# Decoder on one core: the row maxima of the heads of 8 taken off inside the score product

## The reference

```
scores = q @ k.T * scale            # 512 queries x 512 or 77 keys
p      = softmax(scores, axis=-1)   # exp(scores - max) / sum
out    = p @ v
```

## Time and profile before

| | us |
|---|---|
| median of 3 runs | 2002.5 |
| lowest and highest | 2000.7, 2007.37 |
| the profiled execution | 1997.6 |
| its span, first to last instruction | 1995.8 |

### The profile page before, as it was taken

The page is one execution under the profiler, slowest core; times in us unless marked ns, Lnnn a source line. Parts: engine busy times, 40 slices in busy tenths (PEclk is TensorE's granted clock), DMA queues, the critical chain, the costliest instruction groups (busy, mean ns, idle before and its releaser), DMA issues. The chain is left out here.

```text
span 1995.8 us, 23570 instructions
## 1 busy us (share of the span) xinstructions
PE 1566.4 (78%) x8740; PEld 718.1 (36%) x8740; DVE 1134.8 (57%) x2827; ACT 610.3 (31%) x839; POOL 131.8 (7%) x156
## 2 busy tenths in 40 slices
PE   1798659994666888885978997985988479994984
PEld 0332334441233433444433323352436223343342
DVE  5685544446966666644455854545454556744445
ACT  1265332223314023321432651411221124541331
POOL 1000000001000500000000000000000103321000
PEclk9799769996978999996997997886986778997687
DMA  4000000003000000000010000000010000000000
GB/s 187 0 2 1 1 1 0 0 0 124 0 1 1 21 22 2 1 1 1 0 75 18 1 1 0 1 1 1 0 63 0 1 0 1 1 1 1 1 1 11
DMA packets 4081, 27.37 MB, mean 14 GB/s; under 512 B 384, under 2 KB 2432, under 8 KB 2944
## 3 DMA queue, kind: packets, MB, share of 16 engines
q1 hardware_dynamic: 2912, 25.35, 3.2%
q10 hardware_dynamic: 1056, 0.52, 0.1%
HBM read 25.34 MB, written 0.52 MB: 13 GB/s over the span
## 5 line engine op out<-in xcount | busy, mean ns | idle before, releaser
L704 ACT ACTIVATE big<-banks 128x1024 f32<-128x1024 f32 (+2 forms) x320 | 294.2, 958 | 427.8 <-PE banks L507 260.2
L602 DVE TENSOR_REDUCE maxima<-banks 128x1 f32<-128x512 f32 (+4 forms) x640 | 362.5, 603 | 100.9 <-PE banks L476 94.2
L503 PE MATMUL banks<-big 32*128 32x512 f32 (+6 forms) x1280 | 259.5, 656 | 16.8 <-DVE negmaxT L615 16.4
L476 PE MATMUL banks<-big 32*128 32x77 bf16 (+6 forms) x1024 | 161.2, 306 | 30.3 <-DVE maxima L602 18.3
L537 PE MATMUL banks<-big,v_heads 128*9 128x512 f32 (+7 forms) x1024 | 164.3, 585 | 5.8 <-ACT heads_out L657 2.9
L342 POOL TENSOR_TENSOR rstd<-mean_var,minus_half 128x4 f32<-128x4 f32 x46 | 46.9, 1020 | 1645.8 <-DVE mean_var L317 1645.8
L1110 DVE TENSOR_TENSOR big<-big,banks 128x512 f32<-128x512 f32 (+1 forms) x88 | 60.5, 687 | 130.5 <-PE banks L1058 125.2
L1085 ACT ACTIVATE big<-banks 128x512 f32<-128x512 f32 (+1 forms) x120 | 71.7, 597 | 200.6 <-PE banks L1055 200.6
L1068 PE MATMUL banks<-big,moe_weights 128*128 128x512 f32 (+1 forms) x240 | 123.0, 593 | 2.8 <-DVE big L1107 1.5
L476 PEld LDWEIGHTS banks<-big 32*128 32x128 bf16 (+1 forms) x1024 | 58.0, 100 | 166.3 <-DVE maxima L602 102.9
L503 PEld LDWEIGHTS banks<-big 32*128 32x128 f32 (+3 forms) x1280 | 77.9, 187 | 79.6 <-ACT big L704 36.2
(11 more groups left out here) (368 smaller groups left out, 2246.1 us busy)
## 6 DMA issues: line engine op xcount, KB each, us to landing
moe_weights<-in_moe SPq DMA_DIRECT2D x1, 4896.0 KB, 22.1
moe_weights<-in_moe SPq DMA_DIRECT2D x1, 4864.0 KB, 15.0
moe_weights<-in_moe SPq DMA_DIRECT2D x1, 3264.0 KB, 10.6
moe_weights<-in_l3x SPq DMA_DIRECT2D x1, 3072.0 KB, 10.2
late_weights<-in_l2x SPq DMA_DIRECT2D x1, 2048.0 KB, 8.1
moe_weights<-in_l SPq DMA_DIRECT2D x1, 1234.0 KB, 13.2
rows<-in_rows SPq DMA_DIRECT2D x1, 1152.0 KB, 8.1
late_weights<-in_turned SPq DMA_DIRECT2D x1, 1152.0 KB, 17.3
```

Of the source, the lines that this page charges most:

```text
L476: last = nc.tensor.matmul(RING[n % NR][:, x * klen:x * klen + last_key(t)], q[rows, t * P:(t + 1) * P], ks[rows, 0:last_key(t)], start=Tru ...
L503: nc.tensor.matmul(SC[pair % 2][0:size, j % 2, n0:S], ks[rows, i * P:i * P + size], q[rows, n0:S], start=True, stop=False)
L602: nc.vector.tensor_reduce(dst, src, AX_X, ALU.max).then_inc(ring_free.up(), 1)
L704: nc.scalar.activation(E[pair % NEP][0:size, :, n0:S], SC[pair % 2][0:size, :, n0:S], ACT.Exp, scale=scale).then_inc(exp_ready.up(), 1)
```

## The change

Each place of 32 rows gets a ninth row: row 8 of the keys holds ones, row 8 of the queries gets the negative maximum in float32, so the score product itself takes the maximum off. The four `pick` products of each round are gone for heads of 8 (320 products in 80 rounds), and `score_ready` is raised by the second score product of each pair. `negmax` is one DVE instruction that writes float32 into every 32nd column of `c.RW`; the four turned tiles are float32; `move_negmax` adds the whole turned bank to the queries' tile in place instead of copying bfloat16. POOL clears `c.RW` at the start of each such attention, and the first `negmax` of a stage waits for that. The ones come from a biased copy (`ninth`), from padded bias vectors, or, in layer 0's attention, from three strided clears at the start. The other head sizes keep their way.

```diff
@@ row_attention @@
+    room_cleared is a further counter
@@ turn_negmax @@
-        to = RING[n % NR][:, 0:S // 2].bitcast(BF16)
+        to = RING[n % NR] if turned else RING[n % NR][:, 0:S // 2].bitcast(BF16)
         for t in range(ST):
-            last = nc.tensor.transpose(to[:, t * P:(t + 1) * P], c.NM[:, g % 2, t, :], c.ident_bf[:])
+            negmax_tile, unit = (c.RW[:, g % 2, t, :], c.ident) if turned else (c.NM[:, g % 2, t, :], c.ident_bf)
+            last = nc.tensor.transpose(to[:, t * P:(t + 1) * P], negmax_tile, unit[:])
@@ scores @@
-            nc.tensor.matmul(SC[pair % 2][0:size, j % 2, n0:S], ks[rows, i * P:i * P + size], q[rows, n0:S], start=True, stop=False)
-        for j in range(HB):
+            last = nc.tensor.matmul(SC[pair % 2][0:size, j % 2, n0:S], ks[rows, i * P:i * P + size], q[rows, n0:S], start=True, stop=turned)
+            if turned and j % 2:
+                last.then_inc(score_ready.up(), 1)
+        for j in range(0 if turned else HB):
@@ negmax @@
+        if turned:
+            row = c.RW[:, g % 2].rearrange("p t (j w) -> p t j w", j=HB)[:, :, :, 8]
+            if g == 0:
+                dve.wait_ge(room_cleared.sem, room_cleared.at(1))
+            nc.vector.tensor_scalar(row, m, -1.0, None, ALU.mult).then_inc(negmax_ready.up(), 1)
+            return
@@ move_negmax @@
+        if turned:
+            q = queries(*groups[g])
+            nc.vector.tensor_tensor(q, q, RING[n % NR][:, :], ALU.add).then_inc(ring_free.up(), 1)
+            return
@@ POOL's program of row_attention @@
+            if turned:
+                nc.gpsimd.memset(c.RW, 0.0).then_inc(room_cleared.up(), 1)
@@ cross_kv @@
-        bias = None if bk is None else bk[:, k:k + 1]
+        bias = c.ninth[:] if bk is None else bk[:, k:k + 1]
@@ the first block @@
+                nc.vector.tensor_copy(c.ninth[:], c.m("ninth"))
...
-                nc.gpsimd.memset(c.big3(4 * TOK, 4 * TOK), 0.0)
+                key_places = c.big3(4 * TOK, 4 * TOK).rearrange("p (n d) -> p n d", d=32)
+                nc.gpsimd.memset(key_places[:, :, 0:8], 0.0)
+                nc.gpsimd.memset(key_places[:, :, 8], 1.0)
+                nc.gpsimd.memset(key_places[:, :, 9:32], 0.0)
```

More of the change, by code:

```diff
@@ L159 @@
     "moe0": [("w1T", P, L0E * L0HID), ("w3T", P, L0E * L0HID), ("w2T", P, L0E * 3 * P)],
-    "const": [("ident", P, P), ("later", P, P), ("later_t", P, P), ("half_later", P, 2 * P), ("half_ident", P, P // 2), ("pick_id", 96, 32), ("pick", P, 4 * P)],
+    "const": [("ident", P, P), ("later", P, P), ("later_t", P, P), ("half_later", P, 2 * P), ("half_ident", P, P // 2), ("pick_id", 96, 32), ("pick", P, 4 * P), ("ninth", P, 1)],
     "mid": [("iota", P, 32), ("same_head", P, P), ("ctxT", CTX, B * SK), ("L1_WdtT", P, P), ("L1_WBT", P, 16), ("L1_WCT", P, 16), ("L1_A_log", P, 16),
@@ L428, in row_attention @@
     NM = c.NM.rearrange("p z t (j r) -> p z t j r", j=HB)
-    (ring_ready, ring_free, negmax_ready, score_ready, exp_ready, value_ready, out_moved, inverse_ready, masked_ready, cleared,
+    (ring_ready, ring_free, negmax_ready, score_ready, exp_ready, value_ready, out_moved, inverse_ready, masked_ready, cleared, room_cleared,
      dve_step) = (counter(c, n) for n in (
          "ring_ready", "ring_free", "negmax_ready", "score_ready", "exp_ready", "value_ready", "out_moved", "inverse_ready",
-         "masked_ready", "cleared", "dve_step"))
+         "masked_ready", "cleared", "room_cleared", "dve_step"))
     filled, emptied = itertools.count(), itertools.count()
@@ L1924, in decoder @@
         c.pick_id = c.sb("pick_id", [96, 32], BF16)
+        c.ninth = c.sb("ninth", [P, 1])
         c.minus_half = c.sb("minus_half", [P, 8])
@@ L2056, in constants @@
         "half_later": np.concatenate([f > 64 * z + p % 64 for z in range(2)], axis=1),
+        "ninth": p % 32 == 8,
         "half_ident": p % 64 == np.arange(64)[None, :],
@@ L2070, in by_rows, with apart @@
     return w.reshape(k, P, -1).transpose(1, 0, 2).reshape(P, -1)
-def apart(w):
+def apart(w, ninth=0.0):
     out = np.zeros((w.shape[0], HEADS, 32), np.float32)
+    out[:, :, 8] = ninth
     out[:, :, 0:8] = w.reshape(w.shape[0], HEADS, 8)
@@ L2142, in lay_out @@
     for name, n in col_names():
-        v = a[name] if n == 1 or a[name].size > P else apart(a[name][None, :])[0]
+        v = a[name] if n == 1 or a[name].size > P else apart(a[name][None, :], 1.0 if name in ("L1_xattn_bk", "L2_attn_bK") else 0.0)[0]
         if v.shape[0] < P:
```

## The result

The changed kernel took 1984.8 us (median of 4 runs, 1982.7 to 1985.1) and the kernel before 2002.6 in the same comparison (4 runs, 2000.7 to 2007.4): a ratio of 0.9905, 95% interval 0.9887 to 0.9924. Faster, by 17.8 us; the forecast was 1988.7 with a range of 1979 to 2000. The profiled execution took 1985.1, with a span of 1983.3 for 1995.8 and a mean granted clock of 0.862, as before. The two spans differ by 12.5 only, because the profiled execution of the kernel before was 5 us faster than its median and that of the changed kernel was not.

What follows compares the result with a forecast made beforehand. With 512 keys DVE was taken to bound group boundaries and the ACT-PE loop plain rounds; 77-key rounds were nearly gapless on PE. Terms -17.0 (512 keys) and +3.2 (77 keys) gave -13.8, so 1988.7 us, range 1979 to 2000.

Steps and rivals of the forecast that it cites:

- The loop through ACT and PE: Plain 512-key rounds: exponentials need only their own pair, so the loop falls from 3.19 to 2.22 us, under DVE's 2.58.
- A sign that I had named: 512-key rounds: ACT's idle before the exponentials would fall under 0.5 us, from 1.24.
- The group of 512 keys: Four 512-key rounds, score start to next group's score start: 12.34 us for 13.33, a gain of 0.99.
- The first passage: First group-to-group step of a 512-key stage, partly at the low clock: taken to gain 1.0 us.
- Five passages: The steady group-to-group steps of a 512-key stage: taken to gain 5.0 us together.
- the seventh passage: Last group-to-group step of a 512-key stage, a bare chain of maxima, float32 tiles and add: taken to gain 1.05 us.
- rival B, the ring: 512 keys: the three-bank ring makes PE wait for DVE, halving the gain to 0.5 per group; about 1996.7 us, chance 0.15.
- The turned maxima in float32: Four float32 tiles add 0.26 to 0.36 us of PE time per group, covered at 512 keys with 0.05 to spare.
- 77 keys: Short stages: a longer chain to the scores costs 0.21 or 0.32 us a round, 1.6 per stage, +3.2 for two.
- rival C: PE's clock falls within the stages, about 1.9 us more per low round; 15 such rounds give about 2017 us; chance 0.08.
- the argument against it: Claim that the clock would hold because the changed loop leaves PE with smaller gaps, not larger.
- Set-up and POOL: Strided clears at the start and POOL's 0.9 us clear in each stage: hidden or nearly so, taken as 0.

Runs made afterwards that it cites:

- e10: The kernel before plus extra, unused score products ahead of the first turned maxima in all four 77-key attentions, nothing else changed: 1976.5 us, ratio 0.987.
- e9: The changed kernel plus extra, unused score products ahead of the first turned maxima in all four 77-key attentions: 1963.7 us, ratio 0.9838.
- e4: The kernel before, all `pick` products kept, but each pair's put right behind its own score products (heads of 8 only): 1989.8 us, ratio 0.9926.
- e1: The changed kernel with the change kept only in the two 512-key attentions, the 77-key ones in their old way: 1984.1 us, ratio 0.9901.
- e7: The changed kernel with the negative maxima as two bfloat16 rows instead of one float32 row, the add kept: 1993.7 us, ratio 0.9962.
- e6: The changed kernel plus the first group's four score products issued twice more at the start of the two short 77-key stages: 1985.4 us, ratio 0.9911.

## Why the prediction was right, point by point

**The loop through ACT and PE.** Right. The exponentials need only their own pair (at 103.19 they start, while the second pair's products end at 104.01), they follow 1.18 after a round's scores (104.93 to 106.11, forecast 1.1), and with the late signal the loop returns. A sign that I had named failed: ACT's idle time doesn't fall under 0.5 but stays at 0.95 in that round, for DVE and PE now set the pace and ACT has time. One more row of the kernel before bears on the reason that was given, beside the earlier trace rows:

```profile
106.50 0.38 PE L507 MATMUL banks<-negmaxT,pick 32*128 32x512 bf16 x2
```

These are the first pair's `pick` products, and yet the exponential that they signal starts at 107.64, after the second pair's scores (106.98 and 0.59). The Trainium skill ("TensorE: Matmul & The Clock Gate", Part 3) says that matmuls start and end in program order. The wait agrees in respect of the ends; the starts in the records don't (106.50 stands before 106.98, the other way round in the program).

**The group of 512 keys.** Right to 0.02 in the group worked through. Here the whole of layer 0's attention by the starts of the turned maxima; first the kernel before:

```profile
82.79 0.59 PE L488 MATMUL banks<-ident_bf,negmax 128*128 128x128 bf16 x4
...
98.97 0.40 PE L488 MATMUL banks<-ident_bf,negmax 128*128 128x128 bf16 x4
...
165.25 0.40 PE L488 MATMUL banks<-ident_bf,negmax 128*128 128x128 bf16 x4
...
178.53 0.40 PE L488 MATMUL banks<-ident_bf,negmax 128*128 128x128 bf16 x4
```

and the changed one:

```profile
82.56 1.09 PE L492 MATMUL banks<-ident,inverses 128*128 128x128 f32 x4
98.29 0.66 PE L492 MATMUL banks<-ident,inverses 128*128 128x128 f32 x4
...
160.05 0.66 PE L492 MATMUL banks<-ident,inverses 128*128 128x128 f32 x4
171.92 0.66 PE L492 MATMUL banks<-ident,inverses 128*128 128x128 f32 x4
```

The first passage gave 0.45 (16.18 to 15.73) where I took 1.0: at the low clock, which lasts to about 94, the passage was mis-sized. Five passages gave 4.5 (66.28 to 61.76) for 5.0; the seventh passage 1.4 (13.28 to 11.87) for 1.05; what follows, to ACT's last copy, 1.1 for 1.5; the start 0.2. Together 7.7 for 8.5. The order of causes that was named (DVE bounds a group, ACT and PE alternate beneath it) holds; rival B, the ring, doesn't appear.

**The turned maxima in float32.** Right: covered with 512 keys by 0.04, on the path with 77.

**77 keys.** For the rounds at full clock the mechanism and the sum were right; that they would run at full clock was wrong. A round at full clock takes 3.59 or, with turned sums beside it, 3.69; the old way at full clock takes 3.29 in e10 (and 3.39):

```profile
601.17 1.10 PE L511 MATMUL banks<-big 32*77 32x512 f32 x8 [0.26 <-DVE negmaxT L623]
...
604.46 1.12 PE L511 MATMUL banks<-big 32*77 32x512 f32 x8 [0.25 <-DVE negmaxT L623]
```

So 0.30 in either kind, for predicted 0.32 and 0.21. Over a whole stage, from the first to the last scores, e9 takes

```profile
230.56 1.10 PE L515 MATMUL banks<-big 32*77 32x512 f32 x8 [0.78 <-DVE big L637]
...
255.33 1.10 PE L515 MATMUL banks<-big 32*77 32x512 f32 x8 [0.34 <-DVE big L637]
```

24.77, and e10 23.06 (235.76 to 258.82); in the second stage 24.77 and 23.04. That is 1.7 a stage, for a forecast of 1.6. Some luck is in it: the prediction's own terms, four rounds of 0.21 and three or four of 0.32, add up to 1.8 to 2.1, and the first two passages cost only 0.05 each. The +4.0 and +0.4 in the table differ from 1.7 by what lies outside the rounds, where the extra products did not hold the clock. Ahead of the first scores of the first stage e9 took 2.4 more, 1.5 of it in the extra products themselves (3.41 for 1.91 in e10):

```profile
224.66 3.41 PE L488 MATMUL banks<-big 32*77 32x512 f32 x13
```

```profile
226.00:232.00 6.00, 4.51 (x50) 2.24 (x43) 2.60 (x7) 0.30 (x1) 0.00 (x0) 0.81 0.00 0
```

The second view is a window of e9 in this stretch; e10 was at 1.00 from 226 to 232. Behind the last scores of the second stage it was e10 that ran at 0.50, from 628 to 636, and took 1.4 more.

In the profiled execution of the changed kernel the two stages lost 17.0, since their rounds ran at 1.2 GHz. The prediction had named a loss of over 4 us in a stage of 77 keys as a sign of being wrong, and a clock of 1.00 throughout as a sign of being right: both went against it (+9.15 and +7.81, at 0.50). This is rival C, to which I gave 0.08, and it came in the stages that I had not looked at for it. Its price was about right (2.3 a round measured, 1.9 predicted). What was wrong is the argument against it, that PE has smaller gaps in the loop: that holds with 512 keys, where the clock stayed at 1.00, and with 77 keys the chain through DVE's add left PE's gap larger (0.52 ahead of the scores at 239.33, 0.25 at 604.46 in e10). That this gap is what takes the clock down isn't shown: e4 and the second short stage of e1 were low with the old chain. I had read rows of a short stage at full clock only, and the windows of the first long one.

Of the reason behind the low clock I can say only what was tried. It doesn't need the lost `pick` products (e4 has them), nor the longer float32 tiles (e7 turns bfloat16, and is low), nor any part of the change in the stage itself (e1's second short stage). The cause stays open. It is lifted by products in the wait ahead of the stage (e6, e9), after which the same rounds hold 1.00. The Trainium skill (same page, Part 4) says that transposes do not count as activity for the clock; no run here parts that from the rest, for none took the transposes away.

**The total.** 1984.8 for 1988.7, inside the range (by the two spans -12.5 for -13.8), but the total is better than its terms. Outside the four attentions it had nothing, and there the clock of one untouched stage gave 12.8, nearly what the clock in the short stages cost beyond the forecast (17.0 less 3.2). That is luck. With most of the clock's part taken out the change is worth 12.6, for a forecast of 13.8. That, and not the nearness of the total, is what speaks for the sum.

**Set-up and POOL.** Nothing shows: in layer 0's attention the clear of `c.RW` takes 0.95 at 70.85 and is done 10.8 before the first turned maxima. In the short stages it is nearest: in the first one it is done at 223.18, 1.2 before the first negative maxima.

## What to carry to other kernels

When an engine waits, ask first what its signal hangs on and what is queued ahead of the signalling instruction: two thirds of the gain per group came from signalling each pair by its own last product, and half of the long stages' gain was to be had in the old kernel by reordering alone. A step that lengthens a serial chain (here the float32 tiles and the add) is free only where another engine's work covers it; price it in each size of the loop. And before a total is believed, add the difference stage by stage, untouched stages too: here one of them moved by 12.8 us where the total moved by 12.5.

## What the runs showed of the hardware that I had not expected

In these stages the clock tended to stay at the level it had. The rounds with 77 keys keep 0.50 for some 24 us while PE is busy 5.60 of 6 us, and the same rounds keep 1.00 at 5.34 of 6; which of the two it is differs between executions of one program. Eight score products more in a stage (four with heads of 64, twelve with heads of 32), which compute nothing that is used, take 13.6 us off the stage of heads of 32, 10.0 off that of heads of 64, and 26 us off the unchanged kernel (2002.2 to 1976.5). That is twice what the change itself brings, and both together, with the old way for 77 keys, make the fastest kernel of the study, 1962.0.

The kernel before itself ranged from 1996.8 to 2014.6 within one comparison of 25 runs, with mean clocks of 0.863 and 0.853 at the ends. A difference of a few us between two such medians can be the clock of one stage.
